# Layer 1 of a two-layer decoder on one core: a table of its own for each engine's order, in place of one common list of steps

## The reference: what is computed

```python
x = _layernorm(x + _L0_attn_ref(x, ...))              # RWKV mixing
x = _layernorm(x + _L0_xattn_ref(x, ctx_1024, ...))   # cross attention, 16 heads
x = _layernorm(x + _L0_ffn_ref(x, ...))               # 2 shared, 16 routed experts
x = _layernorm(x + _L1_attn_ref(x, ...))              # Mamba-2, 8 heads, state 128
x = _layernorm(x + _L1_xattn_ref(x, ctx_1024, ...))   # mLSTM, 4 heads
x = _layernorm(x + _L1_ffn_ref(x, ...))               # FFN with signs as weights
```

## Time and profile before

| what | us |
|---|---|
| median of 3 runs | 1498.09 |
| the three runs | 1496.36, 1498.09, 1498.52 |
| the profiled execution | 1499.02 |
| its span, first to last instruction | 1497.3 |
| layer 1 in it, 868.9 to the end | 628.4 |
| PE busy in the span | 1273.8 |
| DVE busy | 836.8 |
| ACT busy | 578.4 |

### The profile page before, as it was taken

One profiled execution on the slowest core, in us unless ns is written; L12 is line 12 of the kernel. 1 busy time (PEld: TensorE's weight loads), 2 busy tenths in 40 slices (PEclk: granted clock), 3 DMA queues, 4 the chain that ended last, 5 costly groups with the idle time before them and its releaser, 6 DMA issues.

```text
span 1497.3 us, 22724 instructions
## 1 busy us (share of the span) xinstructions
PE 1273.8 (85%) x8404; PEld 1052.2 (70%) x8404; DVE 836.8 (56%) x2630; ACT 578.4 (39%) x1307; POOL 152.1 (10%) x184
## 2 busy tenths in 40 slices
PE   4899999998998998998989957777878977987866
PEld 3678887676887777886778846565667756876755
DVE  5725378654577464687354766336736472656352
ACT  2246342364322473423554234323423532452333
POOL 4996013000000000000000000000010001000000
PEclk9999799999799997999997978578868975996788
DMA  8000001000001000000101110000100000010000
GB/s 326 20 15 2 1 1 43 16 1 1 1 1 44 15 1 1 1 26 19 59 1 36 36 57 0 1 1 0 29 14 1 20 24 1 0 29 14 1 15 14
DMA packets 21388, 33.27 MB, mean 22 GB/s; under 512 B 11424, under 2 KB 12192, under 8 KB 20128
## 3 DMA queue, kind: packets, MB, share of 16 engines
q1 hardware_dynamic: 21280, 31.82, 6.2%
HBM read 27.62 MB, written 4.19 MB: 21 GB/s over the span
## 4 chain that ended last, share of the span: by engine, by line
PE 68%; DVE 20%; ACT 7%; issue 4%; POOL 1%; DVEq 0%; ACTq 0%; POOLq 0%
PE ps L433 39%; PE ps L676 6%; PE ps L574 3%; DVE arena L1701 3%; PE ps L592 2%; PE ps L591 2%; DVE z L1513 2%; PE ps L590 2%; DVE arena L1330 1%; PE ps L566 1%; PE ps L564 1%; DVE pq L1360 1%; PE ps L537 1%; PE ps L550 1%; ACT pq L1031 1%
## 5 line engine op out<-in xcount | busy, mean ns | idle before, releaser
L433 PE MATMUL ps<-wts,arena 128*128 128x256 f32 (+2 forms) x1008 | 215.7, 375 | 2.2 <-ACT arena L1271 2.2
L433 PE MATMUL ps<-arena,wts 128*128 128x256 f16 (+1 forms) x1344 | 190.6, 297 | 20.6 <-ACTq L406 20.6
L433 PEld LDWEIGHTS ps<-wts,arena 128*128 128x128 f32 (+1 forms) x1008 | 164.8, 166 | 45.3 <-ACT arena L1271 3.0
L433 PEld LDWEIGHTS ps<-arena,wts 128*128 128x128 f16 (+1 forms) x1344 | 154.0, 115 | 49.9 <-issue 20.8
L1513 DVE SCALAR_TENSOR_TENSOR z<-ps,small,z 128x256 f32<-128x256 f32 x256 | 123.8, 484 | 41.3 <-PE ps L676 26.8
L676 PE MATMUL ps<-wts,pq 128*128 128x256 f32 x512 | 121.1, 381 | 4.7 <-DVE z L1513 4.7
L1121 ACT ACTIVATE pq<-ps 128x512 f32<-128x512 f32 x72 | 43.0, 597 | 170.7 <-PE ps L433 170.6
L676 PEld LDWEIGHTS ps<-wts,pq 128*128 128x128 f32 x512 | 92.8, 191 | 17.1 <-DVE z L1513 3.2
L574 PE MATMUL ps<-ident,pq 128*128 128x128 f32 x384 | 73.8, 305 | 32.7 <-DVE arena L1430 11.9
L433 PE MATMUL ps<-xT,wts 128*128 128x256 f32 x320 | 88.0, 430 | 10.0 <-DVE arena L1701 10.0
L574 PEld LDWEIGHTS ps<-ident,pq 128*128 128x128 f32 x384 | 46.9, 160 | 58.0 <-ACT arena L999 26.6
(11 more groups left out here) (286 smaller groups left out, 2488.2 us busy)
## 6 DMA issues: line engine op xcount, KB each, us to landing
cT<-in_cT SPq DMA_DIRECT2D x16, 256.0 KB, 2.8
wts<-in_up SPq DMA_DIRECT2D x1, 2304.0 KB, 15.4
wts<-in_down SPq DMA_DIRECT2D x1, 2304.0 KB, 20.4
xT<-in_xT SPq DMA_DIRECT2D x8, 256.0 KB, 4.1
xin<-in_x SPq DMA_DIRECT2D x8, 256.0 KB, 3.0
xmid<-xin SPq DMA_DIRECT2D x8, 256.0 KB, 2.0
wts<-in_w SPq DMA_DIRECT2D x2, 1024.0 KB, 5.0
wts<-in_c SPq DMA_DIRECT2D x16, 128.0 KB, 3.2
```

The costliest lines, as they stand in the source:

```text
L433: ins = mm(out_, l, r, start=(n == 0), stop=(n == len(pairs) - 1))
```

## The change

`WINDOW`, `FIRST` and `stream()` go. In their place stand five tables, `PE_ORDER`, `ACT_ORDER`, `DVE_ORDER`, `POOL_ORDER` and `SP_ORDER`, each a list of all steps of that engine over all four turns in an order of its own. A step is written as turn.name.arguments, with "-" for the steps that belong to no turn. The amount of computation is the same. What an order could no longer take for granted is now waited for explicitly: PE waits for each of the pairs of channel blocks and not for the last alone (`xs`, `rms`, `out`, `down`), each `in` and `zg` waits for its transposed input, and in the first turn `ztc` and `down` wait for every tile of the transposed signs. DVE's `al2` is parted in two steps, and the negation after `dsum` becomes a step `dcs`, so that other work can stand between. SP's transfers have steps too (`x`, `ctx`, `store`), which wait for the same events as before.

```diff
-STREAM = stream()
-PAIRS = [("Y" if w[1] == "decay" else "H", w[0], w[2], w[3]) for w in STREAM if w[1] in ("decay", "cell")]
+PE_ORDER = steps("""
+    0.load.0 0.load.1 0.in.0.2 0.in.0.0 0.zg.1.2 0.dt.0 -.al2 -.tr.0.1.4 0.zg.0.2 -.tr.1.0.0 -.tr.1.1.0 0.in.1.4
...
+ACT_ORDER = steps("""
+    -.arow -.nw 0.load.0 0.load.1 0.in.0.2 -.al.0 0.in.0.0 -.al.1 0.zg.1.2 -.tr.0.1.4 0.zg.0.2 0.conv.0.2 0.dt.0
...
+DVE_ORDER = steps("""
+    -.al.0 -.al.1 -.al2 0.in.0.2 0.dt.0 -.al2b 0.in.0.0 -.tr.1.0.0 -.tr.1.1.0 -.tr.1.5.0 -.tr.1.2.0 0.dsum.0
...
+PAIRS = [("Y" if w[1] == "decay" else "H", w[0], w[2], w[3]) for w in PE_ORDER if w[1] in ("decay", "cell")]
...
-                eng.wait_ge(*pe.at("conv", s, DM - 2))
+                for m in range(0, DM, 2):
+                    eng.wait_ge(*pe.at("conv", s, m))
...
-            for turn, step, *n in STREAM:
+            for turn, step, *n in PE_ORDER:
...
-                    colproj(s, "xbc", win[:, :, DI:2 * DI + 2 * DS], xT[s], [], m, m + 2, "c")
+                    colproj(s, "xbc", win[:, :, DI:2 * DI + 2 * DS], xT[s], [("zTa", s, "out")], m, m + 2, "c")
...
-                    rowproj(s, "mo", wout, carve_m(s)[3], [("y", s, DM - 2)], spot(RINGS["b"]), kc=DM)
+                    rowproj(s, "mo", wout, carve_m(s)[3], [("y", s, m) for m in range(0, DM, 2)], spot(RINGS["b"]), kc=DM)
...
-                    rowproj(s, "f2", w2T, hTb(s), [("f1", s, FM - 2, "out")], spot(RINGS["b"]), kc=FM)
+                    rowproj(s, "f2", w2T, hTb(s), [("f1", s, m, "out") for m in range(0, FM, 2)], spot(RINGS["b"]), kc=FM)
...
+            def scale_out():
                 eng.wait_ge(*v.at("al2row"))
...
                 if step == "dsum":
                     mamba_sums(s)
+                if step == "dcs":
                     mamba_steps(s)
...
-                if step == "read" and n[1] == LH // 2 - 1 and turn + 1 < 2 * TURNS:
...
+                if step == "ctx":
+                    sp.turn = turn - 1
+                    for pr in range(LH // 2):
+                        eng.wait_ge(*sp.at("H", s, pr))
```

More of the change, by code:

```diff
@@ L61 @@
 SBLK = 3 * P
-LAG = {"M": 0, "X": 1, "F": 2}
-WINDOW = [(w[0],) + tuple(int(x) if x.isdigit() else x for x in w.split(".")[1:]) for w in """
-    M.load.0 X.ztb.0 M.load.1 X.ztb.1 X.gates.0 M.dt.0 X.gates.1 M.dt.1 F.ztc.0 X.forget.0 M.dsum.0 F.ztc.1 X.forget.1
-    M.dsum.1 F.up.0.0 M.in.0.0 X.gain.0 F.up.0.2 M.in.0.2 X.gain.1 M.csrow.0 F.up.0.4 X.rows.0 M.in.0.4 F.up.0.6
-    X.rows.1 M.csrow.1 M.in.1.0 F.up.1.0 F.up.1.2 X.cols.0 M.in.1.2 F.down.0 F.up.1.4 X.cols.1 F.up.1.6 M.in.1.4
-    M.zg.0.0 M.conv.0.0 M.zg.0.2 M.conv.0.2 M.conv.0.4 F.down.1 M.zg.1.0 M.cb.0 M.xs.0 M.conv.1.0 M.zg.1.2 M.conv.1.2
-    M.conv.1.4 X.nrm.0 X.nrm.1 F.ln6.0 X.cell.0.0 X.score.0.0 F.ln6.1 M.cb.1 M.xs.1 M.decay.0.0 X.cell.0.1 X.read.0.0
-    X.score.0.1 M.scan.0.0 M.decay.0.1 X.cell.1.0 X.read.0.1 X.score.1.0 M.scan.0.1 M.sq.0.0 M.decay.0.2 X.hidden.0
-    X.cell.1.1 X.read.1.0 X.score.1.1 M.scan.0.2 M.decay.0.3 X.read.1.1 X.heads.0 M.scan.0.3 M.decay.1.0 X.hidden.1
-    M.sq.0.2 M.decay.1.1 M.scan.1.0 X.ln5.0 M.rms.0 M.decay.1.2 M.scan.1.1 X.heads.1 M.out.0 M.sq.1.0 M.decay.1.3
-    M.scan.1.2 M.ln4.0 X.ln5.1 M.scan.1.3 M.sq.1.2 M.rms.1 M.out.1 M.ln4.1""".split()]
@@ L1195, in _ @@
             eng.wait_ge(*act.at("p2rows"))
-            for turn, step, *n in STREAM:
+            for turn, step, *n in ACT_ORDER:
                 act.turn = turn
@@ L1870, in _ @@
             eng.wait_ge(*v.at("p2rows"))
-            for turn, step, *n in STREAM:
+            for turn, step, *n in DVE_ORDER:
                 v.turn = turn
@@ L1877, in _ @@
                     scale_row()
[L1878 removed]
+                if step == "al2b":
+                    scale_out()
+                if step == "tr":
                     scaled_signs(n[1])
@@ L2014, in _ @@
             eng.wait_ge(*po.at("p2rows"))
-            for turn, step, *n in STREAM:
+            for turn, step, *n in POOL_ORDER:
                 po.turn = turn
```

136 lines of the change are left out of this document (106 added, 30 removed).

## The result

| kernel | median of its runs, us | ratio to before, 95% interval | layer 1 in the profiled run, us | TensorE idle in it, us | granted clock in it |
|---|---|---|---|---|---|
| before | 1497.22 (1493.55 to 1498.52, 4 runs) | 1 | 628.4 | 143.8 | 0.77 |
| after | 1302.29 (1298.92 to 1309.37, 4 runs) | 0.8708 [0.8665, 0.8751] | 428.3 | 26.4 | 0.93 |

The kernel after is 13% faster, with 1302 us where 1364 was predicted and 1312 was the low end of the range. The direction was right; the size was not. What came is nearly the rival "it packs better", to which the prediction gave 0.15: 30 us of idle time, a clock of 0.93, 1306 us. (Its 1306 lies outside of the range that was said to take in most of it.) The profiled run of after took 1298.9 us with a span of 1297.2 us.

The account below looks back on a forecast made before the run. Layer 1 was taken as bound by PE's 373 us of full-clock work, plus low clock and idling. Work at clock 0.87 (429) + idling 60 + waits 5 = 494 us in place of 628.4, giving 1364 us, range 1312 to 1440.

Parts of the forecast that it names:

- it packs better: Whole layer 1: only 30 us of idling and a clock of 0.93, in all 1306 us; chance 0.15.
- The calibration factor of the handoffs: Layer 1, PE steps dependent through ACT and DVE: missing distance 18.0 us, multiplied by 1.5, gives 27 us idle.
- The start: Start of layer 1: abs-sums come first on DVE; 10 us of idling in place of 12.6 and its neighbours.
- DVE and PE side by side: First `dsum` to `ztc` of turn 0: 114 us of PE work, 116 of DVE, no slack; 12 us idle.
- Table loads: ACT in layer 1: 70 loads in place of 14, 71.8 us more, one in seven on the path; 11 us.
- (B): ACT in layer 1: all 71.8 us of added table loads delay the chains, time 1425 us; chance 0.12.
- More waits: PE in layer 1: 108 added explicit waits at 0.05 us each cost 5 us.
- The clock: PE in layer 1: fewer, shorter waits raise the mean clock from 0.77 to 0.87, so its work takes 429 us.
- rival A: Whole layer 1: new order idles only 30 us at clock 0.93, layer 1 436 us, in all 1306; chance 0.15.
- (D): PE in layer 1: spread short waits leave mostly 1.2 GHz, mean clock 0.62, in all 1537 us; chance 0.03.
- (E): All tables: they do nothing, since waiting engines wait for everything in front of the producer's step; 1498 us, chance 0.01.
- (C): Layer 1: two-bank rings and DVE's queue hold PE back, 110 us idle, clock 0.80, in all 1451; chance 0.09.

Follow-up runs that it names:

- tied run: All engines but SyncE walk one common list made from the new TensorE order, against the kernel after's own tables: 1454.47 us, ratio 0.974.
- run with VectorE freed: VectorE alone gets its own order, against the kernel whose engines share one list made from the new TensorE order: 1352.84 us, ratio 0.9058.
- run with two loads: The kernel after with a load of another set ahead of each table load of layer 1: 1361.03 us, ratio 0.9108.
- without loads: The kernel after with SiLU and GELU of layer 1 replaced by the identity, so no table load is left there: 1302.65 us, ratio 0.8694.
- the padding: The kernel after with four more sums in each of 12 VectorE taps steps, in turns 0 and 1 (1324.52 us) or 2 and 3 (1315.03 us).

## Why the prediction missed, step by step

- **What bounds layer 1** was right: TensorE with its work of 373 us (374 measured), idle time and the low clock on top. The handoffs named from the earlier trace rows are the ones that went.
- **The calibration factor of the handoffs** is the step where the reasoning failed. "So the count has to be multiplied by 1.5, because DVE has other work queued in front of the chain's": that queueing is a property of the common list, and it is what the change removes. The tied run shows it, with 5.79 us of taps ahead of a softplus' end; the run with VectorE freed takes 102 us away. Outside of the start and the stretch at par, 26.4 - 2.9 - 4.2 = 19.3 us are idle in after, 13.8 of them at the end. The count without the factor was 18.0, of which 14 in `ztc`, `up` and `down`, mostly at the end. The term was 27, 8 too much. The bare count is no law either: the tied run has nearly the same distances on TensorE and idles for 113.7 us. It met the measured time only where the producers' own orders keep their queues clear.
- **The start**: 10 us forecast, 2.9 measured up to 900 us. The abs-sums do come first on VectorE, but TensorE has enough to do, and its first `decay` stands at 900 us in place of 928.
- **DVE and PE side by side**: 12 us forecast, 4.2 measured between 900 and 1016 us (4.9 from the first `dsum` at 888 us). VectorE is busy for 86% of the time from 930 to 1016 us there, but being at par is not idle time. That this stretch has less slack than the later ones, as the prediction argued, is not shown: the padding costs about its own length in both places.
- **Table loads**: 11 us forecast, none that can be told measured. Doubling them gives 59 us, so the rival (B) was wrong in place and right in kind: the loads do come onto the path somewhere between 70 and 140 of them. In after the 70 loads take 1283 ns each, 89.8 us in all, as the earlier trace rows had them. The Trainium skill (ScalarE: Activation LUTs, section What ACT_TABLE_LOAD costs) adds a drain of about 1380 ns to each; no run here shows one. In after ScalarE stands idle for 1.2 us in all just ahead of the 70 loads, and behind 63 of them the next activation starts within 0.03 us.
- **More waits**: 5 us forecast, none that can be told from zero.
- **The clock**: 0.87 forecast, 0.93 measured. The relation was about right and its input was wrong. The run with two loads has 63.1 us idle and 0.87, just the pair of the forecast; over the runs 143.8, 113.7, 103.0, 102.0, 63.1, 58.8 and 26.4 us of idle time go with 0.77, 0.80, 0.79, 0.81, 0.87, 0.89 and 0.93. It is loose: under 40 us the clock is anywhere from 0.90 to 0.93 (23.9 us and 0.91 without loads), and what kind of product runs counts too, by the 0.97 with 96 columns and the 0.90 with dummies.
- **The sum**: idle time was forecast at 65 with the waits' 5, and is 26.4: 38.6 us, of which the handoffs are 7.7, the start 7.1, the stretch at par 7.8, the loads 11 and the waits 5. All five terms erred to the same side, and none alone carries the miss: without the factor the forecast would have been some 1350 (an estimate: 56 of idle time and a clock of 0.88). The clock term, 373 / 0.87 = 429 against 401.9, is 27 us. Together they are the 66 us between 494 and 428.3; the median stands 5 us over the profiled span of 1297.2, where the prediction added 0.8.
- **The chances**: the forecast's own argument for rival A, that nearly every distance exceeds its chain, was the count itself. Weighed against a factor measured on the order that goes, it deserved more than 0.15. (D) shows nowhere. (E)'s mechanism, that what a producer has in front of it eats the distance, is what the tied run shows; own orders take it away. Of (C) there is a trace: `scan` waits 2.7 us in 2 for a GELU (L1347) whose bank it takes, against the 110 us of idle time that (C) needed.

## What to carry to other kernels

An own order for each engine and a good order on the bottleneck engine brought less than half as much apart (49 and 43 us) as together (195): give the engine whose results are waited for (here VectorE) its own order, and see that the bottleneck has work between a producer and its consumer to use it. When a schedule's idle time is forecast from counted distances, do not scale by what the old schedule lost, since that loss may be part of what goes, but check that the producers' queues are clear, without which the count says nothing; and turn idle time into clock by pairs measured on the same kernel, as a rough guide. Once idle time is gone, look at what TensorE did just ahead of each fall of the clock: products of 1 to 8 columns cost the same as ones of 96 here, and widening them gave about 1% more.

## What the runs showed of the hardware that I had not expected

- A TensorE that is hardly idle can still lose its clock: 4.87, 4.80 and 5.00 us busy in 5 us each, with clocks of 1.00, 0.73 and 0.59, behind 24 products of 8 columns and 16 of one. With 96 columns in the same products the clock of layer 1 was 0.97 in place of 0.93, and 16 products took 2.00 us, where 16 of one column took 2.02.
- 528 dummy products that add 87 us of work to TensorE made the kernel before no slower, ratio 0.99 [0.9847, 0.9954], by a clock of 0.90 in place of 0.77.
- Seventy table loads of 1.283 us, 90 us on ScalarE, cost nothing that can be told from zero, within some 10 us, where ScalarE is busy for 69% of the stretch (295.5 of 428.3 us); the next 90 us cost 59.
